# Gated cross-attention and mixture-of-experts block on one core: maxima rows leave before a wait, and the first expert weights are split one piece per step

## The chip, the core and the metric

The kernel runs on one core of a Trainium2 chip. A core has a matrix engine (TensorE, PE in the tables, with its weight loads as PEld), a vector engine (VectorE, DVE), a scalar engine (ScalarE, ACT), a general engine (GpSimd, POOL) and a queueing engine (SyncE, SP) that here only issues transfers. Every engine works through its own stream of instructions in the order in which they are written; between engines they wait for counting semaphores. The metric is the time of one execution on the device in microseconds; the number compared is the median of several runs.

## The reference

For 16 batches of 128 tokens with 512 features (x) and a context of the same size:

```python
x = x + tanh(g_xattn[0]) * xattn(layernorm(x), ctx, ctx)
x = x + tanh(g_ffn[0])   * ffn(layernorm(x), router, experts, shared expert)

def xattn(q, k, v):          # q, k, v: (16, 128, 512)
    # 8 heads of 16 "channels"; the 512 columns are the positions
    qk = einsum('bdm,bdn->bmn', q16, k16) / sqrt(16)     # 512 x 512 scores per head
    return einsum('bmn,bcn->bcm', softmax(qk), v16)

def ffn(t):                  # 2048 tokens
    combine = renormalised top 4 of softmax(t @ w_router)   # 16 experts of width 256
    moe = sum_e combine_e * (silu(t @ w_gate_e) * (t @ w_up_e)) @ w_down_e
    shared = (silu(t @ w_sh_gate) * (t @ w_sh_up)) @ w_sh_down   # width 1408
    return moe + sigmoid(t @ w_sh_expert_gate) * shared
```

All is float32. To keep the precision with the faster float32r matmuls, operands are split in an upper half (rounded) and a lower half (the rest), and three products replace one.

## The kernel before

Attention comes first, then a second part with the shared chunks and the experts; between the two stands a barrier of all engines (two `nc.Block`s). The change touches attention alone.

Attention goes through 32 groups of four heads (NG = 32), two for each batch. One group is one *slot*; slots 0 to 6 and 27 to 31 are written out, those between are a loop of four slots (`slots`). In slot g PE computes, in the order that a string of letters writes out (`ORDER`, and `LAST_ORDERS` for the last two slots):

- S: scores of groups g + 1 and g + 2 (L815), only for their maxima, which DVE takes (L707);
- M: the transposes of the maxima of group g + 1 (L861) and of its values (L863). The maxima, split by POOL (`split_maxima`, L546 and L548), are so turned into rows, copied by ACT into max_t (L624), and written by a transfer from SP (`store_max_rows`, L395) into two rows of q_stack, so that the scores of the next slot come out with the maximum already taken off;
- T: sixteen score tiles e = 0 to 15 of group g (L842), whose exponentials ACT takes one by one (L658). The first of them waits for the maxima rows (`max_rows`);
- B, C, D, E: products of the exponentials with the values (L853); O: transposes of the outputs (L869);
- L: in even slots the transposes back to rows (L876), in odd slots those of the normalised rows yn of a finished batch (`normed_t`, L882), which wait for `yn_done`, that is POOL's `normed` (L527);
- F, in slots 30 and 31 in place of S: parts of the first products of the first shared chunk (L144), which wait for `w_lo_done`.

The first shared chunk's weights (three pieces of 128 x 512) are loaded by SP (`load_first_chunk`, from slot 28, L113 and L116), their upper halves copied by ACT (`upper_weights`, L639) and their lower halves made by POOL (`lower_weights`, L574).

SP's stream in a slot is: values of a later group; in even slots the finished rows y and yn of an earlier batch out (`keep_y`, L415 and L416) and, once y has landed (`y_kept`), the load of new residual rows x_res (L435) into the same tile; then the maxima rows, which wait for max_t; then the split halves of a prepared batch out (L375) and the stacks of a later group in (L386). Each wait there holds all that stands behind it.

POOL's stream in slot 29 is: residual add of a batch (L554, its wait has long been over), `split_maxima`, then the reciprocal deviation (L517 and L519) and `normed` of batch 13 (L527), then the three `lower_weights`.

Of the kernel before, what the change touches and what calls it, by code (L numbers as in the profile page):

```python
# [149 lines left out]
def gated_block(nc, x, ctx_in, g_xattn, g_ffn, w_router, w_gate, w_up, w_down, ws_gate, ws_up, ws_down, w_eg, out):  # L150
# [5 lines left out]
    HG = 4  # L156
    GR = HG * HD
    NG = B * HEADS // HG
# [8 lines left out]
    with ExitStack() as whole:  # L167
# [192 lines left out]
        @block.sync  # L360
        def _(sp):
            def load_rows(b, j, waits):
                if waits:
                    sp.wait_ge(xn_done, b - 1)
                    sp.wait_ge(k_lo_done, b - 1)
                sp.dma_start(x_in[j], x[b]).then_inc(x_loaded[j], 16)
                sp.dma_start(k_in[j], ctx_in[b]).then_inc(k_loaded[j], 16)

            def store_halves(b, j):
                for dram, tile, parts, done, stored in ((k_dram, k_hi, slice(0, 3, 2), k_hi_done, k_stored), (k_dram, k_lo, slice(1, 2), k_lo_done, k_stored),  # L370
                                                        (q_dram, q_hi, slice(0, 2), q_hi_done, q_stored), (q_dram, q_lo, slice(2, 3), q_lo_done, q_stored)):
                    sp.wait_ge(done, b + 1)
                    dst = dram[b][:, :, parts].rearrange("h e m d -> (h e) m d")
                    src = tile[j].bitcast(F32).rearrange("p (m d) -> p m d", m=1)
                    sp.dma_start(dst, src.to_broadcast([P, dst.shape[1], D]) if dst.shape[1] > 1 else src).then_inc(stored[j], 16)  # L375

            def load_values(j, b, half):
                sp.dma_start(v_rows[j][:, :], ctx_in[b][half * GR:(half + 1) * GR, :]).then_inc(v_loaded[j], 16)

            def load_stack(i, b, half, n):  # L380

                for stack, stored, dram in ((k_stack, k_stored, k_dram), (q_stack, q_stored, q_dram)):
                    sp.wait_ge(stored[half_of_pair(i)], 32 * n + 32)
                    for hf in range(2):
                        src = dram[b][half * HG + 2 * hf:half * HG + 2 * hf + 2].rearrange("h e m d -> (e m) h d")
                        sp.dma_start(stack[i][64 * hf:64 * hf + ROWS, :, :].bitcast(F32), src).then_inc(stack_loaded[i], 16)  # L386

            def half_of_pair(i):
                return i // 2

            def store_max_rows(i, g):

                sp.wait_ge(mt_done, g + 1)
                for hf in range(2):
                    sp.dma_start(q_stack[i][64 * hf + ROWS:64 * hf + ROWS + 2, :, :].bitcast(F32),  # L395
                                 max_t[16 * hf:16 * hf + 16, :].bitcast(F32)).then_inc(max_rows[i], 16)

            for b in range(2):
                load_rows(b, b, False)
            for b in range(2):  # L400
                store_halves(b, b)
                for half in range(2):
                    if b and half:
                        sp.wait_ge(max_rows[0], 32)
                    sp.wait_ge(fixed_rows[2 * b + half], 1)
                    load_stack(2 * b + half, b, half, 0)
                if b == 0:
                    load_values(0, 0, 0)
                    load_values(1, 0, 1)
            load_rows(2, 0, True)  # L410

            def keep_y(b, j, done, n):

                sp.wait_ge(done, n)
                sp.dma_start(y_all[:, bass.ds(b * D, D)], x_res[j][:, :]).then_inc(y_kept[j], 16)  # L415
                sp.dma_start(yn_dram[b], yn[:, :]).then_inc(yn_stored, 16)  # L416

            def load_first_chunk():
                for j in range(2):
                    sp.wait_ge(k_stored[j], 16 * B)  # L420
                    sp.wait_ge(q_stored[j], 16 * B)
                ex.load_chunk(sp, first_chunk, ex.w_loaded)

            def slot(s):
                if s.known() and s.g == NG - 4:
                    load_first_chunk()
                if s.before(NG - 2):
                    sp.wait_ge(vm_done, s.g + 1)
                    load_values(s.q % 2, 2 * s.r + s.q // 2 + 1, s.q % 2)
                if s.q % 2 == 0:  # L430
                    b, j = 2 * s.r + s.q // 2, s.q // 2
                    if s.at_least(4):
                        keep_y(b - 2, j, yn_done, b - 1)
                        sp.wait_ge(y_kept[j], 16 * s.r)
                    sp.dma_start(x_res[j][:, :], x[b]).then_inc(res_loaded[j], 16)  # L435
                if s.before(NG - 1):
                    store_max_rows((s.q + 1) % 4, s.g + 1)
                if prepared(s):
                    store_halves(2 * s.r + 2 + s.q // 2, s.q // 2)
                if s.q % 2 == 1 and s.before(NG - 5):  # L440
                    load_rows(2 * s.r + 3 + s.q // 2, (s.q // 2 + 1) % 2, True)
                if s.before(NG - 4):
                    sp.wait_ge(sb_done, 16 * s.g + 16)
                    load_stack(s.q, 2 * s.r + 2 + s.q // 2, s.q % 2, s.r + 1)

            slots(sp, slot)
            keep_y(B - 2, 0, yn_done, B - 1)
            sp.wait_ge(last_yn, 1)
            sp.dma_start(yn_dram[B - 1], yn[:, :]).then_inc(yn_stored, 16)
            for j in range(2):  # L450
                sp.wait_ge(y_kept[j], 16 * (B // 2 - j))
            sp.wait_ge(yn_stored, 16 * B)
# [3 lines left out]
        def _(pool):  # L456
# [82 lines left out]
            def split_maxima(q, g):  # L539
                whole_max = maxima[q % 2][:, :].rearrange("p (h u) -> p h u", u=8)  # L540
                hi, lo = (max_parts[q % 2][:, :, a, :] for a in range(2))
                pool.wait_ge(max_done, 8 * g + 8)
                if not (isinstance(g, int) and g < 2):
                    pool.wait_ge(vm_done, g - 1)
                pool.sem_inc(pool_waited, 1)
                pool.tensor_copy(hi.bitcast(F32R), whole_max).then_inc(mhi_done, 1)  # L546
                pool.wait_ge(mhi_done, g + 1)
                pool.tensor_tensor(lo, whole_max, hi, ALU.subtract).then_inc(mlo_done, 1)  # L548
# [7 lines left out]
            def slot(s):  # L556
                if has_late(s):
                    residual(batch_late(s), 1 if s.q == 1 else 0, s.r - 1 if s.q == 1 else s.r)
                if s.q % 2 == 0 and s.at_least(4):
                    split_yn(2 * s.r + s.q // 2 - 2)  # L560
                if s.before(NG - 1):
                    split_maxima((s.q + 1) % 4, s.g + 1)
                if prepared(s):
                    prepare(2 * s.r + 2 + s.q // 2, s.q // 2, s.r + 1)
                if has_late(s):
                    reciprocal_deviation(batch_late(s))
                    normed(batch_late(s), 1 if s.q == 1 else 0)
                if s.known() and s.g == NG - 3:
                    for i in range(3):
                        lower_weights(i)  # L570

            def lower_weights(i):
                pool.wait_ge(ex.w_hi_done, i + 1)
# [10 lines left out]
        def _(act):  # L584
# [63 lines left out]
            def slot(s):  # L648
                for e in range(4 * HG):
                    c, j = e // HG, e % HG  # L650
                    if e == VALUES and s.before(NG - 1):
                        values_and_maxima((s.q + 1) % 4, s.g + 1, s.r, VALUES % 3)
                    if place_of_score(s, e) == place_of_turned(s) + 1:
                        turned(s)
                    act.wait_ge(sb_done, 16 * s.g + e + 1)
                    if j == 0 and (c >= 2 or s.at_least(1)):
                        act.wait_ge(pv_done, 4 * s.g + c - 1)
                    act.activation(probs[:, c % 2, head(j)[2], :], sb_ps[:, bank_of_score(s, e), :],  # L658
                                   ACT.Exp, scale=SCALE).then_inc(exp_done, 1)
                    if e == (HG if s.known() and s.g >= NG - 2 else 3) - 1 and s.at_least(1):  # L660
                        copy_out(s.g - 1)
                    if c >= 1 and j == HG - 1 and s.known() and s.g == NG - 3:
                        act.wait_ge(ex.w_loaded, 48)
                        upper_weights(c - 1)
                if place_of_turned(s) == LAST:
                    turned(s)

# [1155 lines left out]
```

## Time and profile before

| | |
|---|---|
| median of 3 runs | 1143.47 us (1143.18 to 1143.86) |
| the profiled execution | 1143.02 us |
| its span in the profile | 1141.3 us |
| PE busy | 1112.0 us, 97% of the span |
| DVE, ACT, POOL busy | 823.6 (72%), 525.9 (46%), 607.5 (53%) |
| attention | to about 433.5 us |

The profile is of one execution. A row of a timeline has its start, its length, the engine and line, the operation, what it writes and reads, and how many instructions are merged in it; in brackets stands the time for which the engine was idle before it and what ended that. Times are microseconds from the start of the span. SPq is SP's queue of transfers; its rows are the issues, not the transfers themselves. Ends of matmuls are modelled, and neighbouring rows overlap a little.

### The profile page before, as it was taken

The numbers are of one execution on the slowest core, as the hardware profiler recorded it, in microseconds if no ns is written. First come the engines' busy times: TensorE is split into PE (matmuls) and PEld (weight loads), VectorE is DVE, ScalarE is ACT, GpSimd is POOL, SyncE is SP. The second block draws the span as 40 slices with busy tenths as digits, with TensorE's granted clock in tenths as the row PEclk, the third lists the DMA queues.
The fourth block names the chain that finished last, engine by engine and source line by source line (L and its number), as shares of the span: only waits on it lengthen the run. The fifth ranks groups of instructions, "written<-read, shape, count | busy, mean of one in ns | idle before, by whom it ended". The sixth has DMA issues, their size and how long they took to land.

```text
span 1141.3 us, 21457 instructions
## 1 busy us (share of the span) xinstructions
PE 1112.0 (97%) x5718; PEld 745.6 (65%) x5719; DVE 823.6 (72%) x1162; ACT 525.9 (46%) x1055; POOL 607.5 (53%) x597
## 2 busy tenths in 40 slices
PE   3999999999999999999999999999999999999998
PEld 1344444444444446887888878888888888878887
DVE  6799999999999607674535476676766767648787
ACT  1588888888888841111111134444444444421110
POOL 3245655565555324035767447566664756238772
PEclk9999999999999999999999999999999999999999
DMA  9568776777767208956465356757567575433665
GB/s 239 150 173 208 206 223 179 207 202 219 201 187 195 76 19 299 398 172 220 143 216 182 139 158 183 226 178 222 182 197 217 175 236 169 147 101 104 182 195 185
DMA packets 138800, 214.34 MB, mean 188 GB/s; under 512 B 16128, under 2 KB 61696, under 8 KB 138752
## 3 DMA queue, kind: packets, MB, share of 16 engines
q1 hardware_dynamic: 107980, 131.10, 39.9%
q0 software_dynamic: 18016, 61.88, 17.2%
q10 hardware_dynamic: 12756, 20.77, 5.4%
q8 instruction: 25, 0.41, 0.1%
q14 instruction: 23, 0.19, 0.1%
HBM read 117.48 MB, written 91.75 MB: 183 GB/s over the span
## 4 chain that ended last, share of the span: by engine, by line
PE 62%; DVE 0%; ACT 0%; issue 0%
PE score_ps L144 21%; PE score_ps L1721 19%; PE d_ps L1747 9%; PE d_ps L1678 8%; PE o_ps L1678 3%; PE d_ps L1735 1%; PE o_ps L1735 1%; PE o_ps L1630 0%; PE o_ps L1633 0%; DVE y_all L1484 0%; PE score_ps L1642 0%; DVE hid L1581 0%; DVE th L1576 0%; PE o_ps L1650 0%; PE o_ps L1649 0%; ACT th L1337 0%
## 5 line engine op out<-in xcount | busy, mean ns | idle before, releaser
L707 DVE TENSOR_REDUCE maxima<-score_ps 128x2 f32<-128x1024 f32 x256 | 305.5, 1218 | 25.9 <-PE score_ps L815 22.6
L658 ACT ACTIVATE probs<-sb_ps 128x512 f32<-128x512 f32 x512 | 271.5, 604 | 75.5 <-PE sb_ps L842 75.1
L144 PE MATMUL score_ps<-yn_t,w_split 128*128 128x512 f32 x1056 | 254.8, 397 | 0.0
L1721 PE MATMUL score_ps<-w_split,x_split 128*128 x948 | 246.8, 398 | 0.0
L144 PEld LDWEIGHTS score_ps<-yn_t,w_split 128*128 128x128 f32 x1056 | 197.0, 188 | 51.4 <-issue 5.4
L1721 PEld LDWEIGHTS score_ps<-w_split,x_split 128*128 128x128 f32 x948 | 172.1, 188 | 32.5
L842 PE MATMUL sb_ps<-q_stack,places 50*128 50x512 f32 x512 | 173.5, 467 | 2.1 <-ACT probs L658 1.2
L815 PE MATMUL score_ps<-places,q_stack 48*128 48x512 f32 x512 | 149.0, 475 | 21.4 <-DMA q_stack<-q_dram 16.2
L1179 POOL CAST w_split<-w_raw 128x1024 fp32r<-128x1024 f32 x63 | 66.8, 1061 | 176.8 <-POOLq L1279 106.8
L1184 POOL TENSOR_TENSOR w_split<-w_raw,w_split 128x1024 fp32r<-128x1024 f32 x63 | 153.7, 2440 | 4.1
L842 PEld LDWEIGHTS sb_ps<-q_stack,places 50*128 50x128 f32 x512 | 77.8, 188 | 112.7 <-ACT probs L658 96.5
L853 PE MATMUL o_ps<-probs,v_t 128*17 128x512 f32 x1024 | 137.4, 609 | 0.0
L1747 PE MATMUL d_ps<-w_split,h_rows 128*128 x474 | 120.3, 389 | 0.0
L815 PEld LDWEIGHTS score_ps<-places,q_stack 48*128 48x128 f32 x512 | 70.0, 195 | 71.7 <-issue 49.4
L1237 POOL DMA_INDIRECT ring<-res_dram,pos x64 | 73.8, 1153 | 59.0 <-DMA res_dram<-stage 36.6
L1747 PEld LDWEIGHTS d_ps<-w_split,h_rows 128*128 128x128 f32 x474 | 88.9, 188 | 18.6
L1303 ACT ACTIVATE h_split<-hid 128x512 fp32r<-128x512 f32 x44 | 27.8, 633 | 158.5 <-DVE hid L1514 152.5
L1678 PE MATMUL d_ps<-w_split,h_split 128*128 128x512 f32 x396 | 94.5, 391 | 0.0
L1228 POOL DMA_INDIRECT xs_dram<-stage,pos x64 | 64.0, 999 | 43.7 <-issue 26.4
L1324 ACT ACTIVATE stage<-d_ps 128x512 f32<-128x512 f32 x79 | 47.4, 600 | 86.3 <-PE d_ps L1747 84.9
L1678 PEld LDWEIGHTS d_ps<-w_split,h_split 128*128 128x128 f32 x396 | 74.2, 188 | 16.2 <-issue 0.2
L1299 ACT ACTIVATE th<-score_ps 128x512 f32<-128x512 f32 x44 | 26.2, 595 | 125.1 <-PE score_ps L144 91.7
(155 smaller groups left out, 1224.0 us busy)
## 6 DMA issues: line engine op xcount, KB each, us to landing
xs_dram<-zero SPq DMA_DIRECT2D x1, 20224.0 KB, 58.6
res_dram<-stage ACTq DMA_DIRECT2D x79, 256.0 KB, 2.3
places<-k_dram SPq DMA_DIRECT2D x64, 192.0 KB, 3.6
q_stack<-q_dram SPq DMA_DIRECT2D x64, 192.0 KB, 4.0
stage<-xs_dram SPq DMA_DIRECT2D x160, 64.0 KB, 2.3
h_split<-xs_dram SPq DMA_DIRECT2D x156, 64.0 KB, 2.4
k_dram<-places SPq DMA_DIRECT2D x16, 512.0 KB, 2.9
q_dram<-places SPq DMA_DIRECT2D x16, 512.0 KB, 3.9
```

Of the source, the lines that this page charges most:

```text
L144: mm = pe.matmul(dst[i], w[:, k, f * P:(f + 1) * P], self.yn_t[:, b, k, t * self.SPAN:(t + 1) * self.SPAN], start=(k == 0 and n == 0), sto ...
L658: act.activation(probs[:, c % 2, head(j)[2], :], sb_ps[:, bank_of_score(s, e), :], ACT.Exp, scale=SCALE).then_inc(exp_done, 1)
L707: dve.tensor_reduce(maxima[q % 2][:, :].rearrange("p (h u) -> p u h", u=8)[:, u, :], sa_ps[:, pair_of_unit(q, g, u), :, :], AX_X, ALU.max) ...
L815: mm = pe.matmul(sa_ps[:, pair, hf, :], q_stack[i][rows, u // 4, at:at + P], k_stack[i][rows, u // 4, :], start=True, stop=True)
L842: pe.matmul(sb_ps[:, bank_of_score(s, e), :], k_stack[s.q][rows, p, c * P:(c + 1) * P], q_stack[s.q][rows, p, :], start=True, stop=True).t ...
L853: mm = pe.matmul(o_ps[32 * j:32 * j + HD + 1, :], v_t[q % 2][:, c, j, 0:HD + 1], probs[:, c % 2, j, :], start=(c == 0), stop=(c == KC - 1))
L1179: pool.tensor_copy(hi, w_raw[:, i * ex.PIECE:(i + 1) * ex.PIECE]).then_inc(w_hi_done, 1)
L1184: pool.tensor_tensor(lo, w_raw[:, i * ex.PIECE:(i + 1) * ex.PIECE], hi.bitcast(F32), ALU.subtract).then_inc(w_lo_done, 1)
L1237: pool.indirect_dma_start(out=ring[i][:, :], out_offset=None, in_=res_dram[:, :], in_offset=bass.IndirectOffsetOnAxis(ap=pos[:, n:n + 1], ...
L1678: mm = pe.matmul(d_ps[i][:, :], h_split[t % 2][:, a, f, i * P:(i + 1) * P], w[:, f, :], start=(n == 0), stop=(n == 3 * c.tiles - 1))
L1721: mm = pe.matmul(gu_ps[j], x_split[j][:, b, k, :], w_split[:, bass.ds(at + (a * 3 * ex.PIECE + k * 2 * FE), 2 * FE)], start=(n == 0), stop ...
L1747: mm = pe.matmul(o_ps[j][:, :], h_rows[j][:, a, f, :], w_split[:, bass.ds(at + (b * 3 * ex.PIECE + 2 * ex.PIECE + f * D), D)], start=(n == ...
```

## The change

On SP, in every slot, the maxima rows now go out between `keep_y` and the wait for `y_kept` with the load of x_res; the load of the first chunk's weights goes, in slot 28, behind these maxima rows and in front of that wait. On ACT the upper halves of the three weight pieces are taken after the third and fourth quarter of slot 29 and the third quarter of slot 30 (before: after the second, third and fourth quarter of slot 29). On POOL the first two lower halves stand right behind `split_maxima` in slots 29 and 30, in front of the reciprocal deviation and `normed`; the third stands at the end of slot 30.

```diff
@@ SP @@
             def slot(s):
-                if s.known() and s.g == NG - 4:
-                    load_first_chunk()
                 if s.before(NG - 2):
                     sp.wait_ge(vm_done, s.g + 1)
                     load_values(s.q % 2, 2 * s.r + s.q // 2 + 1, s.q % 2)
@@
                     if s.at_least(4):
                         keep_y(b - 2, j, yn_done, b - 1)
+                if s.before(NG - 1):
+                    store_max_rows((s.q + 1) % 4, s.g + 1)
+                if s.known() and s.g == NG - 4:
+                    load_first_chunk()
+                if s.q % 2 == 0:
+                    if s.at_least(4):
                         sp.wait_ge(y_kept[j], 16 * s.r)
                     sp.dma_start(x_res[j][:, :], x[b]).then_inc(res_loaded[j], 16)
-                if s.before(NG - 1):
-                    store_max_rows((s.q + 1) % 4, s.g + 1)
@@ POOL @@
                 if s.before(NG - 1):
                     split_maxima((s.q + 1) % 4, s.g + 1)
+                if s.known() and NG - 3 <= s.g < NG - 1:
+                    lower_weights(s.g - NG + 3)
                 if prepared(s):
                     prepare(2 * s.r + 2 + s.q // 2, s.q // 2, s.r + 1)
                 if has_late(s):
                     reciprocal_deviation(batch_late(s))
                     normed(batch_late(s), 1 if s.q == 1 else 0)
-                if s.known() and s.g == NG - 3:
-                    for i in range(3):
-                        lower_weights(i)
+                if s.known() and s.g == NG - 2:
+                    lower_weights(2)
@@ ACT @@
-                    if c >= 1 and j == HG - 1 and s.known() and s.g == NG - 3:
+                    if c >= 2 and j == HG - 1 and s.known() and s.g == NG - 3:
                         act.wait_ge(ex.w_loaded, 48)
-                        upper_weights(c - 1)
+                        upper_weights(c - 2)
+                    if c == 2 and j == HG - 1 and s.known() and s.g == NG - 2:
+                        upper_weights(2)
```

## Rows read from the trace of the kernel before

**Rows 1.** Windows: start:end, length, busy PE, PEld, DVE, ACT, POOL; clock, DMA share, GB/s.
```profile
336.00:348.00 12.00, 11.99 (x82) 5.09 (x82) 10.92 (x13) 9.94 (x22) 6.79 (x9) 1.00 0.71 172
386.50:431.00 44.50, 43.26 (x243) 18.71 (x241) 9.91 (x16) 23.34 (x45) 11.45 (x14) 1.00 0.08 31
```

**Rows 2.** Timeline, PE, slots 27 to 30: start, length, line, count, [idle before <-releaser].
```profile
359.24 0.27 PE L861 MATMUL sb_ps<-ident,max_parts 128*32 128x128 f32 x1
...
370.82 0.27 PE L861 MATMUL sb_ps<-ident,max_parts 128*32 128x128 f32 x1
...
377.28 0.50 PE L842 MATMUL sb_ps<-q_stack,places 50*128 50x512 f32 x1 [0.19 <-DMA q_stack<-max_t]
...
382.76 0.27 PE L861 MATMUL sb_ps<-ident,max_parts 128*32 128x128 f32 x1
...
384.03 0.49 PE L842 MATMUL sb_ps<-q_stack,places 50*128 50x512 f32 x1 [0.32 <-ACT probs L658]
...
386.52 0.66 PE L882 MATMUL sb_ps<-ident,yn 128*128 128x128 f32 x4
...
390.11 0.50 PE L842 MATMUL sb_ps<-q_stack,places 50*128 50x512 f32 x1 [0.20 <-ACT probs L658]
```

**Rows 3.** Timeline, POOL, slot 29.
```profile
379.97 0.22 POOL L548 TENSOR_TENSOR max_parts<-maxima,max_parts 128x16 f32<-128x16 f32 x1
...
381.38 0.19 POOL L517 TENSOR_TENSOR var_eps<-mean_var,eps 128x1 f32<-128x1 f32 x1 [1.19 <-DVE mean_var L729]
...
382.45 2.08 POOL L527 TENSOR_SCALAR yn<-x_res,mean_var,rstd 128x512 f32<-128x512 f32 x1 [0.24 <-POOL rstd L519]
...
386.41 1.28 POOL L574 TENSOR_TENSOR w_split<-w_raw,w_split 128x512 fp32r<-128x512 f32 x1 [0.62 <-ACT w_split L639]
```

**Rows 4.** Timeline, ACT, slots 27 to 30.
```profile
360.38 1.53 ACT L658 ACTIVATE probs<-sb_ps 128x512 f32<-128x512 f32 x3
...
371.52 0.27 ACT L624 ACTIVATE max_t<-sb_ps 32x128 fp32r<-32x128 f32 x1
...
384.29 1.52 ACT L658 ACTIVATE probs<-sb_ps 128x512 f32<-128x512 f32 x3
...
385.72 0.61 ACT L639 ACTIVATE w_split<-w_raw 128x512 fp32r<-128x512 f32 x1
...
387.36 0.60 ACT L636 ACTIVATE yn<-sb_ps 128x512 f32<-128x512 f32 x1
...
400.91 2.15 ACT L658 ACTIVATE probs<-sb_ps 128x512 f32<-128x512 f32 x4 [1.70 <-PE sb_ps L842]
```

**Rows 5.** Timeline, SP's queue, slots 27 and 28.
```profile
357.30 0.56 SPq L378 DMA_DIRECT2D v_rows<-in_ctx_dram  x1
...
360.23 1.30 SPq L395 DMA_DIRECT2D q_stack<-max_t  x2
...
368.24 0.60 SPq L415 DMA_DIRECT2D y_all<-x_res  x1
...
374.07 0.34 SPq L435 DMA_DIRECT2D x_res<-in_x_dram  x1
...
374.45 1.37 SPq L395 DMA_DIRECT2D q_stack<-max_t  x2
```

**Rows 6.** DMA issues between 360 and 380 us: queue, count, KB, median us to landing.
```profile
w_raw<-in_L_ffn_w_sh_down_dram SPq DMA_DIRECT2D x1, 256.0 KB, 5.8
```

**Rows 7.** Timeline, DVE and PE, the end of attention.
```profile
430.41 0.55 DVE L786 TENSOR_SCALAR yn<-y_all,mean_var,rstd 128x512 f32<-128x512 f32 x1 [0.95 <-POOL rstd L519]
...
431.16 0.66 PE L882 MATMUL sb_ps<-ident,yn 128*128 128x128 f32 x4
...
433.54 2.35 PE L1630 MATMUL o_ps<-yn_t,w_r 128*32 128x512 f32 x21 [1.73 <-PEq L982]
```

**Rows 8.** Timeline, PE, slot 1.
```profile
47.83 1.91 PE L853 MATMUL o_ps<-probs,v_t 128*17 128x512 f32 x8
...
51.41 1.05 PE L853 MATMUL o_ps<-probs,v_t 128*17 128x512 f32 x8
```

## The prediction

> **What bounds the kernel now.** I read the page's busy shares first, then the busy time by stretches, then the instructions in order of time on TensorE (PE), ScalarE (ACT), GpSimd (POOL) and SyncE's queue (SP) for the last slots of attention. The reader is to see that PE is the busiest engine of the page, and is busy 11.99 of 12.00 us in a slot of attention [rows 1]. PE's waits stand in its stream in a fixed order, so every moment that it waits in attention is added to the span: nothing else there has to be caught up with. In the same slot ACT is busy 9.94 us, VectorE (DVE) 10.92, POOL 6.79 [rows 1]: none is the bound, but each has moments at which PE needs its answer.
>
> A slot is one group of four heads. Between the transposes of the maxima of slots 27 and 28 lie 370.82 - 359.24 = 11.58 us, between those of 28 and 29 382.76 - 370.82 = 11.94, 0.36 more [rows 2]. In that stretch PE waited at 377.28 for the maxima rows (DMA into q_stack). Slot 29 holds the step on which I think everything hangs: PE's transposes of the normalised batch (L882) at 386.52 [rows 2]. They wait for yn_done, that is for POOL's yn, which ran from 382.45 for 2.08 us and was ready at 384.53, two microseconds early [rows 3].
>
> **Part 1: maxima rows in front of the wait for y_kept (SP).** In slot 28 the maxima were ready on ACT at 371.52 + 0.27 = 371.79 [rows 4]; SP issued their rows only at 374.45, because it sat until 374.07 in the wait for the kept y (issued 368.24) before it could load x_res [rows 5]. That transfer was slow because the first chunk's weights (up to 5.8 us to landing) went out just before it [rows 6]. After the change the rows go out at about 371.8 + 0.1 and the weights behind them. They land some 2.5 us earlier than at 377.28, and PE's wait goes: **-0.36 us**, the whole excess of that slot over 11.58. What is late next there is nothing: slot 27 to 28 is the same code without the wait. Bounds: 0 to -0.36.
>
> In all other even slots the rows go out at most some tenths earlier and PE did not wait for them: 0. In exchange x_res leaves about 1.4 us later and the stores of the halves about 0.5 us later, on SP's queue. What hides it: in the next odd slot SP has issued its last load at 357.30 and then sits idle until the maxima at 360.23, over 2 us of slack for everything moved [rows 5]. x_res is read three slots later. If that cover were gone, the rows of one slot would come 0.5 us later and would still be ahead of PE's first use of them, which in slot 28 came 377.28 - 371.79 = 5.5 us after they were ready. Taken: 0, bounds -0.1 to +0.4 over all slots.
>
> **Part 2: the weights land later.** Their three loads move from before the loads of slot 28 to after its maxima rows, 371.9 + 1.4 = 373.3 to about 374.7. With the slowest landing of before, 5.8 us [rows 6], they are there by 380.5. ACT first asks for them now after exponential e = 11 of slot 29, at about 385. Cost 0. Without that cover each microsecond of lateness beyond 385 would be one on PE.
>
> **Part 3: ACT's upper halves one step later.** Before: after e = 7, 11, 15 of slot 29. Now: after e = 11 and 15 of slot 29 and e = 11 of slot 30. The one after e = 7 goes; it was 0.6 us of ACT in front of the maxima's copy. The one in slot 30 falls where ACT, done with e = 11, waited 1.70 us for PE before the exponentials at 400.91 [rows 4]: cover for 0.61, cost 0.
>
> When is the first upper half ready? In slot 27 the exponentials 9 to 11 ended at 360.38 + 1.53 = 361.91, which is 2.67 after PE's transposes at 359.24 [rows 2, 4]. In slot 29 of the new kernel those transposes are at 382.76 - 0.36 = 382.40, so e = 11 ends at 385.07. The upper half starts 0.09 before that end, as it did at 385.72 behind exponentials that ended at 384.29 + 1.52 = 385.81, and takes 0.61: **ready at 385.59** [rows 4].
>
> **Part 4: POOL's lower halves move in front of yn.** This is the costly one. In slot 29 POOL now does: maxima parts (done at 379.97 + 0.22 = 380.19), then lower_weights(0), and only then the reciprocal deviation and yn [rows 3]. lower_weights(0) waits for ACT's upper half, so POOL stands still from 380.2 to 385.6 with the whole normalisation queued behind it. Then: start 385.59 + 0.08 = 385.67 (the 0.08 is 386.41 less 385.72 + 0.61), 1.28 us, end 386.95 [rows 3, 4]. From the start of the reciprocal deviation (381.38) to the end of yn (384.53) POOL took 3.15 us [rows 3]; from 386.92 that gives 390.07. PE's transposes of a yn began 0.20 us after it was written at the end of attention (431.16 against 430.41 + 0.55) [rows 7], so **L882 starts at 390.27 instead of 386.52: +3.75 us**. Part 1's gain and the ACT time freed in part 3 are inside this figure: they make PE reach the step sooner (at about 385.8) and wait longer, some 4.4 us, and the only way in which they count is that e = 11 ends earlier.
>
> What is queued behind the waiting PE: the last scores of slot 29, the products with the values, all of slot 30. ACT gives back a little. Before, its copy of the transposed yn came at 387.36, 0.84 after L882 began, held by exponentials; now it has caught up and is held by PE alone, and in the stretch after it PE waited 0.20 us for ACT, at 390.11, behind an upper half of the same length as the one that stands there now [rows 2, 4]. I take 0.15 back, bounds 0 to 0.20. In slot 30 POOL does its remaining two lower halves in front of nothing that PE asks for soon: the second needs 1.28 us and PE's second product of the first chunk comes a whole third of a slot after POOL is free; the third is first read in the down products after attention. 0.
>
> **Sum.** +3.75 - 0.15 + 0 = +3.6 us. The profiled execution's own time was 1143.02 (its span 1141.3, 1.7 around it), so it would take 1146.6; against the median of the runs, 1143.47, I predict **1147.1 us**. About 0.2% (2.3 us) is what a measurement of this kernel tells from no change; this is 0.31%.
>
> **The rivals.**
>
> *A. The clock falls in the gap.* After slot 1 PE's longest wait is 1.73 us, where attention ends [rows 7], so the trace does not show what a gap of 4.4 us does. At the start it shows the lower level: a group of eight matmuls (L853) took 1.91 us at 47.83 and 1.05 at 51.41 [rows 8], 1.2 against 2.4 GHz, although PE had been nearly always busy since 36 us. So coming back can take long. If the gap drops the clock, c us at the lower level cost about c/2. With the stretch from 36 to 51 as the length, c = 15: +7.5, in all +11.1, 1154.6; with a third of it, 1149.6. For it: the long idle stretch before the start ended in a slow one. Against it: the gap is short beside that one, and the granted clock reads 1.00 from 386.5 to 431 with all its small waits [rows 1].
> The Trainium skill ("TensorE: Matmul & The Clock Gate", Part 1 on the HAM clock gate) says that idleness puts the array back to 1.2 GHz and that sustained activity releases it; by that rule this rival is a real possibility, where the rows alone only show that the slow level exists at the start. No row of before shows a fall after a gap. Chance 0.14.
>
> *B. The delay is given back before attention ends.* From 386.5 to 431 PE was busy 43.26 of 44.50 us [rows 1], so 1.24 us of waiting are all there is to absorb, and those waits (ACT's answers to PE's own work) shift along with it. All of it absorbed would give +3.6 - 1.24 = +2.4, 1145.8, and 1145.4 with the 0.4 us by which single runs lie off their median. Chance 0.08.
>
> *C. Not slower.* The mechanism: PE reaches L882 after yn anyway. It decides at yn ready by about 385.8, POOL starting yn's chain at 382.5, so ACT's first upper half done by 381.2. Then only the gains count: -0.36 in slot 28, and 0.32 in slot 29, where PE waited for ACT at 384.03 behind the upper half that goes [rows 2]: 1143.47 - 0.7 = 1142.8. Against it: in the code that half comes behind e = 11, and e = 11's scores come behind the maxima's transposes at 382.4. Chance 0.05.
>
> *D. Weights or queued loads on the path.* If the weights' landing ran past 385, by two microseconds say, because values, x_res and kept rows share the queue with them, L882 would come at 392.3: +5.6, 1149.1. Against: 4.5 us of slack. Chance 0.03.
>
> The forecast keeps 0.70; its own range is 1146.3 to 1147.8.
>
> **Range and chances.** Low 1145.4 takes in B. High 1150.5 takes in D and the short form of A; outside are C and the long forms of A. Slower by over 0.2%: the forecast, A, D and a little of B, 0.88. Within: most of B and part of C, 0.09. Faster by over 0.2%: 0.03.
>
> **What would show it.** In the new profile: L882 of slot 29 3.75 us later than 386.52, with POOL's lower half (L574) from about 385.7 and yn from about 388.0 in front of it; a hole of some 4 us on PE, the largest after slot 1; POOL waiting over 5 us for ACT at the first L574; no wait of PE for the maxima rows at 377; the distance between maxima transposes of slots 28 and 29 back at 11.58 and that of 29 and 30 longer by 3.9. Every later stage is to keep its length. I am wrong if yn is ready before PE asks, if the matmuls after the gap take twice as long (A), or if the first slots or the expert tiles change length.

## The result, and the profile after

| | before | after |
|---|---|---|
| median, runs on one chip | 1143.12 us (6 runs, 1140.4 to 1143.86) | 1147.32 us (6 runs, 1145.95 to 1148.46) |
| ratio | | 1.0040 (95% interval 1.0026 to 1.0054) |
| the profiled execution | 1143.02 us | 1148.40 us |
| its span | 1141.3 us | 1146.7 us |
| granted clock, mean | 1.000 | 0.997 |

The predicted time was 1147.1 us. The change is slower, by 4.2 us in the medians and 5.4 in the profiles. Ratios, here and below, are formed from the fast runs alone (a run over 1.5% above the fastest counts as slow) and need not equal the quotient of the two medians. Line numbers moved: L861 is now L866 (transposes of the maxima), L882 is L887 (transposes of yn), L853 is L858, L527 is L529, L639 is L642.

The timeline of PE after the change, slots 27 to 31, answers to [rows 2, 7]:

```profile
358.70 0.27 PE L866 MATMUL sb_ps<-ident,max_parts 128*32 128x128 f32 x1
...
370.29 0.27 PE L866 MATMUL sb_ps<-ident,max_parts 128*32 128x128 f32 x1
...
376.40 0.64 PE L847 MATMUL sb_ps<-q_stack,places 50*128 50x512 f32 x2
...
381.80 0.27 PE L866 MATMUL sb_ps<-ident,max_parts 128*32 128x128 f32 x1
...
384.89 0.40 PE L820 MATMUL score_ps<-places,q_stack 48*128 48x512 f32 x2
389.57 1.08 PE L887 MATMUL sb_ps<-ident,yn 128*128 128x128 f32 x4 [4.28 <-POOL yn L529]
...
391.74 1.91 PE L858 MATMUL o_ps<-probs,v_t 128*17 128x512 f32 x8
...
395.48 1.05 PE L858 MATMUL o_ps<-probs,v_t 128*17 128x512 f32 x8
...
401.24 0.27 PE L866 MATMUL sb_ps<-ident,max_parts 128*32 128x128 f32 x1
...
436.07 0.66 PE L887 MATMUL sb_ps<-ident,yn 128*128 128x128 f32 x4
```

The reader is to see three things. Behind 376.40 there is no wait for the maxima rows any more. At 389.57 PE has waited 4.28 us for POOL's yn. And the first group of eight products behind that wait takes 1.91 us, the second 1.05. The distances between these marks, before and after, are the whole account:

| from | to | before | after | difference |
|---|---|---|---|---|
| start | maxima of slot 27 | 359.24 | 358.70 | -0.54 |
| maxima 27 | maxima 28 | 11.58 | 11.59 | 0.01 |
| maxima 28 | maxima 29 | 11.94 | 11.51 | -0.43 |
| maxima 29 | transposes of yn | 3.76 | 7.77 | +4.01 |
| transposes of yn | maxima 30 | 9.79 | 11.67 | +1.88 |
| maxima 30 | last transposes of yn | 34.85 | 34.83 | -0.02 |
| last transposes of yn | end of span | 710.1 | 710.6 | +0.5 |

The -0.54 of the first row is not the change: the maxima transposes of the third group already come at 55.45 us in this profile and at 56.00 in that of the kernel before. That is the clock's first rise, which moves from execution to execution (see the open points).

POOL and ACT after, slots 28 and 29, against [rows 3, 4]:

```profile
379.44 0.22 POOL L550 TENSOR_TENSOR max_parts<-maxima,max_parts 128x16 f32<-128x16 f32 x1
385.06 1.26 POOL L577 TENSOR_TENSOR w_split<-w_raw,w_split 128x512 fp32r<-128x512 f32 x1 [5.41 <-ACT w_split L642]
386.28 0.19 POOL L519 TENSOR_TENSOR var_eps<-mean_var,eps 128x1 f32<-128x1 f32 x1
...
387.35 2.08 POOL L529 TENSOR_SCALAR yn<-x_res,mean_var,rstd 128x512 f32<-128x512 f32 x1 [0.24 <-POOL rstd L521]
```

```profile
370.99 0.27 ACT L627 ACTIVATE max_t<-sb_ps 32x128 fp32r<-32x128 f32 x1
...
382.94 1.53 ACT L661 ACTIVATE probs<-sb_ps 128x512 f32<-128x512 f32 x3
384.37 0.61 ACT L642 ACTIVATE w_split<-w_raw 128x512 fp32r<-128x512 f32 x1
...
390.69 0.60 ACT L639 ACTIVATE yn<-sb_ps 128x512 f32<-128x512 f32 x1 [4.52 <-PE sb_ps L887]
```

POOL stood still for 5.41 us in front of its first lower half, until ACT's upper half (384.37 + 0.61), and only then came the deviation and yn, ready at 387.35 + 2.08 = 389.43. SP's queue, against [rows 5]: the maxima rows leave at 371.28, 0.02 after ACT's copy ended, the weights behind them.

```profile
371.28 1.37 SPq L395 DMA_DIRECT2D q_stack<-max_t  x2
372.82 0.40 SPq L113 DMA_DIRECT2D w_raw<-in_L_ffn_w_sh_gate_dram  x1
...
374.36 0.43 SPq L439 DMA_DIRECT2D x_res<-in_x_dram  x1
```

The term that was not in the sum shows in the granted clock (busy time by stretches; the last four columns are granted clock, DMA share and GB/s):

```profile
386.00:388.00 2.00, 0.00 (x0) 0.00 (x0) 0.56 (x1) 0.17 (x1) 1.69 (x4) 1.00 0.00 0
388.00:390.00 2.00, 0.43 (x2) 0.46 (x3) 0.00 (x0) 0.00 (x0) 1.43 (x1) 0.52 0.00 0
390.00:392.00 2.00, 2.00 (x12) 0.91 (x14) 0.16 (x1) 1.17 (x3) 0.54 (x1) 0.50 0.66 252
392.00:394.00 2.00, 2.00 (x10) 0.43 (x4) 1.07 (x1) 1.03 (x3) 1.34 (x2) 0.50 0.03 10
394.00:396.00 2.00, 2.00 (x16) 0.72 (x14) 1.13 (x1) 1.60 (x4) 0.00 (x0) 0.77 0.00 0
396.00:398.00 2.00, 2.00 (x14) 0.78 (x6) 1.22 (x2) 1.87 (x4) 0.50 (x3) 1.00 0.00 0
```

PE did nothing in 386 to 388; from 388 on the granted clock is 0.50, 1.2 GHz of 2.4, until in 394 to 396 it comes back.

### The profile page after: what moved, and what is told of

Read it like the earlier page. It is cut to its first block, busy times and chain, and to the rows that moved or that the text cites. A ratio compares the mean times of both kernels' runs of the same rounds, so it can differ in the third digit from the quotient of the medians.

```text
span 1146.7 us, 21457 instructions
## 1 busy us (share of the span) xinstructions
PE 1114.1 (97%) x5718; PEld 746.0 (65%) x5719; DVE 819.4 (71%) x1162; ACT 526.1 (46%) x1055; POOL 606.2 (53%) x597
## 4 chain that ended last, share of the span: by engine, by line
PE 61%; DVE 1%; ACT 0%; issue 0%
PE score_ps L144 20%; PE score_ps L1726 19%; PE d_ps L1752 9%; PE d_ps L1683 8%; PE o_ps L1683 3%; PE d_ps L1740 1%; PE o_ps L1740 1%; DVE col L1394 0%; PE o_ps L1635 0%; PE o_ps L1638 0%; DVE h_split L1526 0%; DVE y_all L1489 0%; DVE th_gate L1393 0%; DVE th L1513 0%; DVE hid L1519 0%
## 5 line engine op out<-in xcount | busy, mean ns | idle before, releaser
L144 PE MATMUL score_ps<-yn_t,w_split 128*128 128x512 f32 x1056 | 254.6, 397 | 0.0
L144 PEld LDWEIGHTS score_ps<-yn_t,w_split 128*128 128x128 f32 x1056 | 197.0, 188 | 51.1 <-issue 5.0
L858 PE MATMUL o_ps<-probs,v_t 128*17 128x512 f32 x1024 | 138.2, 612 | 0.0
L1752 PEld LDWEIGHTS d_ps<-w_split,h_rows 128*128 128x128 f32 x474 | 88.9, 188 | 18.5
```

What stands on the lines that cost most here:

```text
L144: mm = pe.matmul(dst[i], w[:, k, f * P:(f + 1) * P], self.yn_t[:, b, k, t * self.SPAN:(t + 1) * self.SPAN], start=(k == 0 and n == 0), sto ...
L858: mm = pe.matmul(o_ps[32 * j:32 * j + HD + 1, :], v_t[q % 2][:, c, j, 0:HD + 1], probs[:, c % 2, j, :], start=(c == 0), stop=(c == KC - 1))
L1752: mm = pe.matmul(o_ps[j][:, :], h_rows[j][:, a, f, :], w_split[:, bass.ds(at + (b * 3 * ex.PIECE + 2 * ex.PIECE + f * D), D)], start=(n == ...
```

## The experiments

All in rounds beside runs of the kernel before. The column "wait" is PE's wait for yn, "to 30" the distance from the transposes of yn to the maxima transposes of slot 30, both in the kernel's profile, as in the table above.

| kernel | median (runs) | before | ratio (95%) | wait | to 30 |
|---|---|---|---|---|---|
| e1_after_again | 1152.10 (6) | 1143.16 | 1.0085 (1.0069 to 1.0100) | 4.28 | 11.82 |
| e7_after_third | 1149.47 (12) | 1143.72 | 1.0037 (1.0004 to 1.0071) | 4.28 | 11.77 |
| e2_keep_busy | 1146.12 (12) | 1143.16 | 1.0031 (1.0015 to 1.0046) | 1.45 | 9.62 |
| e4_upper_early | 1145.19 (12) | 1143.16 | 1.0019 (1.0006 to 1.0032) | 1.52 | 10.95 |
| e3_yn_first | 1142.39 (12) | 1143.16 | 0.9992 (0.9979 to 1.0005) | none | 9.77 |
| e10_yn_first_again | 1142.43 (12) | 1143.41 | 0.9994 (0.9981 to 1.0007) | none | 9.79 |
| e5_sp_only | 1143.29 (12) | 1143.72 | 0.9986 (0.9953 to 1.0019) | none | 9.81 |
| e6_engines_only | 1154.05 (12) | 1143.72 | 1.0078 (1.0046 to 1.0109) | 4.28 | 16.55 |
| e8_warm_start | 1145.75 (12) | 1143.72 | 1.0011 (0.9987 to 1.0035) | none | 9.80 |
| e9_warm_more | 1142.08 (12) | 1143.41 | 0.9985 (0.9971 to 1.0000) | none | 9.78 |

**The changed kernel again, twice.** No edit.

> The changed kernel itself, as the yardstick of this group. Theory (PE's wait for yn plus the lower clock behind it): the wait of about 4.3 us in front of L887 and some 6 to 7 us at the lower clock level behind it, in all 4 to 5.5 us slower than the kernel before (1147 to 1148.5 us). Rival (the extra over 3.6 us comes from elsewhere, the start or the expert part): the same time, but the profile has no stretch at the lower clock in this run.

> The changed kernel a third time, beside its parts. Theory: 4 to 6 us above the kernel before; the extra over 3.4 us is the stretch at the lower clock behind the wait, 2 us. Rival (the second group's 9 us was the change): 8 us or more again.

Their profiles are copies of the first one: 11.51 us from maxima 28 to 29, 7.77 and 7.76 to the transposes of yn, 11.82 and 11.77 from there to slot 30. The profiled executions took 1148.87 and 1148.48 us. The other runs spread from 1148.06 to 1154.63 us, one at 1169.38, and the difference of the medians was 8.9 and 5.8 us. So the first expectation (4 to 5.5 us) was missed in the median, though its profile has the wait and the lower clock that the theory named. By the marks the change costs 5.61 and 5.55 us in these two profiles (-0.43 + 4.01 + 2.03 and -0.43 + 4.00 + 1.98); the 8.9 us did not come back, and the third group's interval still holds 3.6 us.

**PE kept busy during the wait.** In front of the wait for yn in slot 29:

```diff
+                            if s.known() and s.g == NG - 3:
+                                for n in range(24):
+                                    pe.transpose(sb_ps[:, bank_of_turned(s), (n % 4) * P:(n % 4 + 1) * P], ident[:, :], ident[:, :])
                             normed_t(batch_late(s), bank_of_turned(s), yn_done, batch_late(s) + 1)
```

> The changed kernel with 24 extra transposes of the identity (3.3 us of PE work) in front of the wait for yn in slot 29, into the bank that the real transposes then overwrite. Theory (the clock falls because PE stands idle): the transposes of yn start where they did (389.6), the clock stays at 1.00, and the time is 1.5 to 2.0 us below the changed kernel's. Rival (the clock is not tied to the idle stretch, or the slow stretch costs nothing that ends late): no difference beyond 0.3 us.

```profile
385.99 2.84 PE L964 MATMUL sb_ps<-ident 128*128 128x128 f32 x24
390.28 0.66 PE L887 MATMUL sb_ps<-ident,yn 128*128 128x128 f32 x4 [1.45 <-POOL yn L529]
...
391.54 1.05 PE L858 MATMUL o_ps<-probs,v_t 128*17 128x512 f32 x8
...
399.90 0.27 PE L866 MATMUL sb_ps<-ident,max_parts 128*32 128x128 f32 x1
```

```profile
388.00:392.00 4.00, 2.55 (x24) 1.44 (x22) 0.36 (x1) 1.03 (x3) 2.34 (x2) 1.00 0.14 51
```

The fillers took 2.84 us, and 1.45 of waiting was left. yn came 7.71 us after the maxima transposes as before, the granted clock stayed at 1.00, and the stretch to slot 30 took 9.62 us instead of 11.67 to 11.82: the lower clock costs **2.05 to 2.20 us**, and in this profile it is gone when most of the idle time is filled. The other executions have no trace, but their mean granted clock is on record: 5 of the 12 read 1.000, where none of the 24 executions of the changed kernel (three groups) reads above 0.998. Three of the twelve read 0.997 and one 0.991; runs of the kernel before read 0.995 to 0.997 as well at times, so where the clock fell in those is not known. The median is 6.0 us below the changed kernel's of the same group, more than this one stretch explains. The profiled execution itself was not shorter (1148.80): its part behind attention took 712.4 us against 710.6, so the step is read from its own stretch and not from the span. What is left, 1146.12 against 1143.16, is 3.0 us, near the 3.41 that wait, maxima rows and what ACT gives back add up to below.

**yn first.** POOL's first lower half behind the normalisation:

```diff
-                if s.known() and NG - 3 <= s.g < NG - 1:
-                    lower_weights(s.g - NG + 3)
                 if prepared(s):
...
                     normed(batch_late(s), 1 if s.q == 1 else 0)
+                if s.known() and s.g == NG - 3:
+                    lower_weights(0)
                 if s.known() and s.g == NG - 2:
+                    lower_weights(1)
                     lower_weights(2)
```

> The changed kernel with POOL's first lower half behind the normalisation in slot 29 instead of in front of it, and the second in slot 30; SP and ACT as changed. Theory: yn is ready at about 384, PE does not wait for it, the clock stays, and the two gains are left (0.36 for the maxima rows, about 0.3 for ACT's upper half that went): 0.4 to 0.8 us below the kernel before, about 1142.4. Rival (moving the weights' load or the upper halves costs as well): at or above the kernel before.

> The kernel with yn first once more, to narrow its ratio. Theory: 0.4 to 0.8 us below the kernel before, no wait of PE for yn. Rival: equal to the kernel before or above it, because PE's short waits in slot 31 can let the clock fall as well.

```profile
380.62 0.27 PE L867 MATMUL sb_ps<-ident,max_parts 128*32 128x128 f32 x1
...
384.05 0.66 PE L888 MATMUL sb_ps<-ident,yn 128*128 128x128 f32 x4
...
393.82 0.27 PE L867 MATMUL sb_ps<-ident,max_parts 128*32 128x128 f32 x1
```

The transposes of yn come 3.43 us after those of the maxima, 0.33 sooner than the 3.76 of the kernel before: that is ACT's upper half that no longer stands in front. The wait and the lower clock behind it are gone with this one order. The medians are 0.8 and 1.0 us below those of the kernel before, but both intervals of the ratio hold 1, so a gain is not shown. Both profiles also have what the rival named: in slot 31 the clock fell, here about 2 us after the end of a wait of 0.68 us. That the wait is the cause is not shown: the same wait of 0.68 or 0.69 us stands in all twelve profiles, and the clock fell behind it in five.

```profile
412.41 0.50 PE L848 MATMUL sb_ps<-q_stack,places 50*128 50x512 f32 x1 [0.68 <-ACT probs L662]
...
415.60 1.91 PE L859 MATMUL o_ps<-probs,v_t 128*17 128x512 f32 x8
```

```profile
414.00:416.00 2.00, 2.00 (x8) 0.85 (x11) 0.00 (x0) 0.60 (x1) 0.00 (x0) 0.59 0.00 0
416.00:418.00 2.00, 2.00 (x11) 0.44 (x3) 0.00 (x0) 0.00 (x0) 0.00 (x0) 0.56 0.00 0
```

From the maxima of slot 30 to the last transposes of yn this took 36.36 us (430.18 less 393.82) against 34.85: 1.5 us, in a stretch that took 34.83 in the changed kernel.

**The upper half early.** ACT as in the kernel before, the rest as changed:

```diff
-                    if c >= 2 and j == HG - 1 and s.known() and s.g == NG - 3:
+                    if c >= 1 and j == HG - 1 and s.known() and s.g == NG - 3:
                         act.wait_ge(ex.w_loaded, 48)
-                        upper_weights(c - 2)
-                    if c == 2 and j == HG - 1 and s.known() and s.g == NG - 2:
-                        upper_weights(2)
+                        upper_weights(c - 1)
```

> The changed kernel with ACT's upper halves where the kernel before had them (after the second, third and fourth quarter of slot 29); POOL's lower half still in front of yn. Theory (PE's wait is the time at which the first upper half is ready, plus 1.28 plus 3.15 us, less PE's own arrival): upper half ready at about 383.1, yn at 387.6, L887 at 387.8, a wait of 1.3 to 1.7 us and no fall of the clock: 1.0 to 1.4 us above the kernel before. Rival (POOL's order alone costs it all, whenever the upper half comes): as slow as the changed kernel, within 1 us.

```profile
380.05 0.27 PE L864 MATMUL sb_ps<-ident,max_parts 128*32 128x128 f32 x1
...
385.39 0.63 PE L885 MATMUL sb_ps<-ident,yn 128*128 128x128 f32 x4 [1.52 <-POOL yn L529]
...
386.83 1.91 PE L856 MATMUL o_ps<-probs,v_t 128*17 128x512 f32 x8
...
390.58 1.05 PE L856 MATMUL o_ps<-probs,v_t 128*17 128x512 f32 x8
```

The wait was 1.52 us, inside the 1.3 to 1.7 that the sum of the theory gave: PE's wait follows the time of the upper half. That the clock would hold was wrong. It fell to 1.2 GHz behind this wait too, from before 386.83 to before 390.58, and the stretch to slot 30 took 10.95 us, 1.3 over 9.62. The median is 2.0 us above the kernel before, where 1.0 to 1.4 were expected. The length of the wait alone does not decide on the fall: behind the 1.45 us left in e2_keep_busy the clock stayed up, and of the twelve executions here three have a mean granted clock of 1.000.

**The parts of the change alone.** First the kernel before with the new order on SP only (the SP hunk of the change).

> The kernel before with the SP part of the change alone: maxima rows in front of the wait for y_kept and of the weights' load; ACT and POOL as before. Theory (the rows were the only late thing there): the distance between the maxima transposes of slots 28 and 29 falls from 11.94 to 11.50 us, the weights still land before ACT asks for them after the second quarter of slot 29, L882 waits for nothing: 0.3 to 0.5 us below the kernel before. Rival (loads and stores pushed back by the rows cost in the loop, or the weights come late for the second quarter): no gain, or PE or ACT waits for a transfer in slot 29 and the time rises by up to 2 us.

```profile
370.91 0.27 PE L863 MATMUL sb_ps<-ident,max_parts 128*32 128x128 f32 x1
...
382.43 0.27 PE L863 MATMUL sb_ps<-ident,max_parts 128*32 128x128 f32 x1
...
386.17 0.66 PE L884 MATMUL sb_ps<-ident,yn 128*128 128x128 f32 x4
```

11.52 us instead of 11.94, no wait for a transfer, the rest of attention as before (3.74, 9.81): the 0.42 us are the SP part's, and in all ten profiles with the new order on SP this distance is 11.49 to 11.52 us. The ratio, 0.9986 (0.9953 to 1.0019), can't tell them from nothing. Then the ACT and POOL hunks only.

> The kernel before with the ACT and POOL parts of the change alone; SP as before. Theory (the whole loss is POOL's lower half in front of the normalisation): 11.94 us stay between the maxima transposes of slots 28 and 29, PE waits 4.3 us for yn, a stretch at the lower clock follows: 4.5 to 6 us above the kernel before. Rival (the loss needs the later load of the weights, because POOL's or ACT's wait ends with a transfer): less than 1 us above.

```profile
388.19 1.08 PE L885 MATMUL sb_ps<-ident,yn 128*128 128x128 f32 x4 [4.28 <-POOL yn L527]
...
394.41 1.91 PE L856 MATMUL o_ps<-probs,v_t 128*17 128x512 f32 x8
...
401.27 1.91 PE L856 MATMUL o_ps<-probs,v_t 128*17 128x512 f32 x8
404.74 0.38 PE L864 MATMUL sb_ps<-ident,max_parts 128*32 128x128 f32 x1
```

```profile
388.00:392.00 4.00, 3.81 (x16) 1.37 (x16) 1.23 (x1) 2.20 (x4) 1.88 (x3) 0.50 0.47 147
392.00:396.00 4.00, 4.00 (x20) 1.27 (x16) 2.36 (x2) 2.08 (x4) 0.05 (x1) 0.50 0.13 49
396.00:400.00 4.00, 4.00 (x12) 1.92 (x9) 0.00 (x0) 2.38 (x5) 1.65 (x3) 0.50 0.00 0
400.00:404.00 4.00, 4.00 (x13) 1.13 (x13) 0.00 (x0) 0.46 (x2) 0.00 (x0) 0.50 0.00 0
404.00:408.00 4.00, 4.00 (x22) 2.33 (x26) 0.68 (x2) 2.87 (x7) 0.00 (x0) 0.88 0.04 8
```

The wait is the same 4.28 us and ends with POOL's yn as before, so the SP part has no share in it. But here the clock stayed at 0.50 for some 16 us, although PE was busy from 388.19 on, and the way to slot 30 took 16.55 us, 6.9 over 9.62. The runs of this kernel go from 1145.94 to 1159.93 us, the median 10.3 above the kernel before, where I expected 6 at most. The long stretch does not explain this median: only four of the twelve runs have a mean granted clock of 0.991 or 0.992 like the profiled one; the other eight read 0.995 to 0.997 and still go up to 1156.00 us. One expectation failed: the 11.94 us between the maxima of slots 28 and 29 were 11.50 here (380.43 less 368.93), with the old order on SP. The rows left at 372.13, 2.23 us after ACT's copy (369.90), against 2.66 in the kernel before, and just made it. So the old order loses 0.4 us in one of its two profiles, not always.

**A start at the higher clock.** On top of yn first, transposes of the identity before the first stacks arrive and after each of the first twelve units of scores (36 and 2, then 56 and 4; the diff is cut, its comments give the numbers of the second kernel):

```diff
+            warm(36)                       # 56 in the second
             pe.wait_ge(s_const, 9)
...
                 for half in range(2):
                     scores(0, 0, 0, u, half)
+                warm(2)                    # 4 in the second
```

> The kernel with yn first, and 36 transposes of the identity on PE while it waits for the first stacks, and two after each of the first twelve units. It leaves nothing out. Theory (the clock starts at its lower level and rises by PE's own activity): the first group of eight matmuls L853 takes 1.05 us instead of 1.91, the maxima transposes of the third group come at 50 to 52 instead of 54 to 56 us, and the time is 3 to 6 us below the kernel before. Rival (the clock's rise is not brought forward by this): the clock rises near 50 us as before and the time is that of the kernel with yn first, within 0.5 us.

> As the kernel with warm start, with 56 transposes of the identity before the first stacks instead of 36, and four after each of the first twelve units instead of two. It leaves nothing out. In the warm start's profile the clock rose near 11.6 us and fell again near 18.5, behind a wait of 2.58 us between the last extra transpose and the first scores. Theory (a wait of that length is what let it fall): the clock stays at 1.00 from about 12 us on, the third maxima transposes come at 50 to 52 us, 3 to 6 us below the kernel before. Rival (the units of the first 30 us do not hold the clock, with fillers or without): it falls again before 30 us, and the time is at or above the kernel before.

The first was a miss: the clock rose, fell again near 18.5 us, some 2.5 us after the end of a wait of 2.58 us, and the third maxima transposes came at 57.48 instead of 56.00. In the second it held longer, and fell in slot 0:

```profile
24.00:32.00 8.00, 7.07 (x44) 4.07 (x42) 8.00 (x8) 0.93 (x3) 0.42 (x2) 1.00 0.49 146
32.00:40.00 8.00, 6.81 (x28) 2.37 (x25) 5.17 (x7) 4.79 (x11) 1.64 (x4) 0.58 0.75 180
40.00:48.00 8.00, 7.19 (x27) 3.06 (x31) 5.05 (x5) 3.98 (x9) 5.31 (x6) 0.50 0.66 231
```

Its third maxima transposes came at 55.45, where 50 to 52 were expected: the clock was held for the first 32 us and not beyond. Nor did it buy much there: the first maxima transposes came at 26.83 us against 26.96 in the kernel before. DVE, which takes the maxima, was busy 8.00 of 8.00 us from 24 to 32. The median is 1.3 us below the kernel before, the lowest of all, with 1.0000 as the upper end of its interval, so no version is clearly shown to beat the kernel before.

## Why the prediction was right, and where it was not

**Part 1 (-0.36).** Measured -0.43 in the profile and -0.42 in the part alone. Right in mechanism for the profile it was read from, and 0.07 us beyond the bound that I had set (the slot came out at 11.51 us, below the 11.58 that I took as its floor); e6_engines_only shows that it is not there in every execution.

**Parts 2 and 3 (0).** Right. The weights landed 4.6 us or less after their issue at 372.8 to 373.8, six microseconds before ACT asked for them. The upper half was ready at 384.98, 3.18 after the maxima transposes at 381.80; 385.59 - 382.40 = 3.19 was predicted.

**Part 4.** From the maxima transposes to those of yn 390.27 - 382.40 = 7.87 us were predicted, 7.77 measured. Of the 0.10, 0.06 are the step from POOL's write to PE: 0.14 here (389.57 less 389.43), 0.20 in the row I took, which was behind DVE. 0.03 are the way from the upper half to the deviation, 1.30 us (384.98 to 386.28) where I had 1.33, and 0.01 lies in front of it. Given back: 0.15 predicted, 9.79 - 9.62 = 0.17 in the profile where the clock stayed up. Together -0.43 + 4.01 - 0.17 = +3.41, where I had +3.6.

**The step that failed is rival A.** I gave 0.14 to a fall of the clock in the gap and left it out of the sum. It fell in all three profiles of the changed kernel, for 2.05 to 2.20 us, and in the two others that have PE wait for yn without fillers, for 1.3 and 6.9 us. Its price was taken from the long slow start, +2.5 to +7.5; the common case was just below that, and the longest, 6.9, inside. With it the sum is 3.41 + 2.05 = 5.46, which is what the marks of attention show (4.01 + 1.88 - 0.43). The Trainium skill ("TensorE: Matmul & The Clock Gate", Part 1 on the HAM clock gate) was the better guide here than the rows that I set against it: idleness brought 1.2 GHz. On the way back this case does not bear it out: it says that sustained activity releases the clock, and in e6_engines_only it stayed at 0.50 from 388 to 404 us with PE busy. What these runs add is that the clock also fell behind 1.52 us of waiting, in one profile, and in slot 31 about 2 us after a wait of 0.68 that left it up in seven others.

**The match of the medians is partly luck.** 1147.1 against 1147.32 has an error of -2 us in the mechanism, made good by the spread of the runs, and for 0.35 us by the median of the kernel before, 1143.12 where I had reckoned from 1143.47: in this group the medians lie 4.2 apart where the profiles lie 5.4, in the others 8.9 and 5.8. Rivals B, C and D did not come. Nothing was given back before attention ended (34.83 against 34.85), yn was never ready first, no transfer was late.

**Open.** Runs of the very same kernel before spread from 1138.8 to 1146.7 us in one group and up to 1158.5 in another. The profiles show three places that move by themselves: the clock's first rise (the third maxima transposes lie between 53.69 and 56.25 us in the profiles without warm start, with nearly the same work in front); the fall in slot 31, worth 1.5 us, there in five of the twelve profiles, among them all four in which the third maxima transposes come before 54.3; and the part behind attention, which took 710.0 to 712.8 us. The falls of the clock that the profiler records do not make the spread. Every execution has its mean granted clock on record, and of the kernel before 15 of the 23 runs in the group from 1138.82 to 1146.72 us read 1.000, the fastest and the slowest among them. In e1_after_again three of six runs read 0.991 to 0.994, so the lower clock lasted longer there than in the profile, but the slowest, 1154.63 us, reads 0.998. So the 8.9 us of that group, and most of the spread, stay open.

## What to carry to other kernels

Before a step is moved ahead of another on an in-order engine, ask when its own input is ready: here a job of 1.26 us, whose result PE first asks for in slot 30 (L144 at 397.12), was put in front of one that PE asked for at 385.29, and its wait of 5.41 us, far more than its own work, became the cost. A wait on TensorE that was not there before can have two prices, its length and what the lower clock takes behind it, 1.3 to 6.9 us here behind waits of 1.52 and 4.28, and nothing behind one of 1.45. Measure such a step by the distances between marks of one stretch; a total that moves by 4 us from run to run hides it.

## What was not expected of the hardware

- PE's clock fell to 1.2 GHz behind a wait of 1.52 us (e4_upper_early) and in slot 31 behind one of 0.68 (five of twelve profiles), and it stayed down for 3.5 to 16 us while PE had work all the time (granted clock 0.50 from 388 to 404 us in e6_engines_only). In the kernel before waits of up to 1.73 us left it up, the same 0.68 in slot 31 among them.
- In the first 50 us the clock column of the kernel before reads 1.00, but the same eight products take 1.91 us at 47.83 and 1.05 at 51.41 [rows 8]. The column did not show the slow start in this profile, nor does the mean of 1.000; the lengths of like instructions are the surer sign.
